# Second self attention of a two-layer transformer kernel: ScalarE seeds the shifted-score banks with the negated maxima, and each fourth slot's score pair stands ahead of its shifted scores

## What is computed

```
q = (h @ wq).reshape(b, n, 16, 64).transpose(0, 2, 1, 3)      # k and v likewise
scores = einsum('bhnd,bhld->bhnl', q, k) * 64 ** -0.5
probs = softmax(scores, axis=-1)
out = einsum('bhnl,bhld->bhnd', probs, v)
return out.transpose(0, 2, 1, 3).reshape(b, n, 1024) @ wo + bo
```

## Time and profile before

| | us |
|---|---|
| runs: median (lowest to highest) | 4218.95 (4212.62 to 4226.44) |
| profiled execution, first to last instruction (its span) | 4217.9 |
| TensorE busy in matmuls | 3909.5 |
| VectorE busy | 2770.9 |
| ScalarE busy | 1839.2 |
| GpSimd busy | 1859.2 |

### The profile page before, as it was taken

One profiled execution on the slowest core, in us unless ns is written; L12 is line 12 of the kernel. 1 busy time (PEld: TensorE's weight loads), 2 busy tenths in 40 slices (PEclk: granted clock), 3 DMA queues, 4 the chain that ended last, 5 costly groups with the idle time before them and its releaser, 6 DMA issues. The chain is left out here.

```text
span 4217.9 us, 64445 instructions
## 1 busy us (share of the span) xinstructions
PE 3909.5 (93%) x24639; PEld 2598.3 (62%) x24639; DVE 2770.9 (66%) x4547; ACT 1839.2 (44%) x2746; POOL 1859.2 (44%) x1203
## 2 busy tenths in 40 slices
PE   3799999994998997998999999999999979999899
PEld 2533443433557886884666666666666647777787
DVE  6599999953536654435676767676766737665665
ACT  1267777771443333442333333333333334444333
POOL 1288970001203002005777777877787753222200
PEclk9789999996779998997999999999999989999899
DMA  4734434405622005883211111121112010000100
GB/s 159 180 56 77 59 57 48 42 2 94 102 43 52 22 13 197 306 308 103 75 51 51 64 63 51 51 76 51 51 51 76 26 31 10 10 10 1 42 15 17
DMA packets 314421, 294.96 MB, mean 70 GB/s; under 512 B 133420, under 2 KB 237292, under 8 KB 313860
## 3 DMA queue, kind: packets, MB, share of 16 engines
q1 hardware_dynamic: 311460, 281.88, 25.7%
q0 software_dynamic: 2656, 8.97, 0.7%
HBM read 161.92 MB, written 127.28 MB: 69 GB/s over the span
## 5 line engine op out<-in xcount | busy, mean ns | idle before, releaser
L1741 POOL TENSOR_TENSOR f_sums<-f_sums,f_probs 128x1024 f32<-128x1024 f32 x384 | 915.5, 2384 | 154.8 <-ACT f_probs L1860 117.1
L1860 ACT ACTIVATE f_probs<-f_st 128x1024 f32<-128x1024 f32 x512 | 525.0, 1027 | 938.7 <-PE f_st L1906 933.9
L1758 DVE TENSOR_REDUCE f_mx<-f_s 128x1 f32<-128x512 f32 x1024 | 659.8, 686 | 380.7 <-PE f_s L1883 369.4
L1369 DVE TENSOR_REDUCE f_mx<-f_s 128x1 f32<-128x512 f32 x1024 | 638.6, 683 | 50.8 <-PE f_s L1501 28.4
L1481 ACT ACTIVATE f_probs<-f_st 128x512 f32<-128x512 f32 x1024 | 535.9, 601 | 225.6 <-PE f_st L1518 225.5
L1883 PE MATMUL f_s<-f_k,f_q 64*128 64x512 f32 x3072 | 515.0, 415 | 18.6 <-DMA f_k<-k 12.5
L1906 PE MATMUL f_st<-f_q,f_k 64*128 64x512 f32 x3072 | 485.2, 390 | 1.1 <-ACT f_probs L1860 1.0
L1920 PE MATMUL f_acc<-f_probs,f_v 128*64 128x512 f32 x2048 | 465.0, 596 | 0.0
L1883 PEld LDWEIGHTS f_s<-f_k,f_q 64*128 64x128 f32 x3072 | 341.2, 189 | 166.6 <-issue 112.1
L1906 PEld LDWEIGHTS f_st<-f_q,f_k 64*128 64x128 f32 x3072 | 366.4, 184 | 25.9 <-ACT f_probs L1860 3.8
L1518 PE MATMUL f_st<-f_q,f_k 50*128 50x512 f32 x1024 | 332.7, 472 | 6.9 <-ACT f_probs L1481 6.8
(11 more groups left out here) (320 smaller groups left out, 7874.5 us busy)
## 6 DMA issues: line engine op xcount, KB each, us to landing
q<-f_stage SPq DMA_DIRECT2D x80, 512.0 KB, 2.9
k<-f_stage SPq DMA_DIRECT2D x80, 512.0 KB, 2.9
f_q<-q SPq DMA_DIRECT2D x32, 1024.0 KB, 5.0
f_k<-k SPq DMA_DIRECT2D x32, 1024.0 KB, 7.3
v<-f_v_stage SPq DMA_DIRECT2D x64, 256.0 KB, 3.1
f_v<-v SPq DMA_DIRECT2D x32, 512.0 KB, 8.5
f_q<-q SPq DMA_DIRECT2D x96, 128.0 KB, 4.2
f_k<-k SPq DMA_DIRECT2D x96, 128.0 KB, 6.9
```

Source lines behind the costliest of these rows:

```text
L1369: v.tensor_reduce(mx[:, i % 2, c:c + 1], bank[u % 4][:, :], AX_X, ALU.max).then_inc(s_free, 1)
L1741: g_.tensor_tensor(out, out, probs[:, n % NP, :, :], ALU.add).then_inc(sum_done, 1)
L1758: v.tensor_reduce(mx[:, i % 2, c:c + 1], bank[u % 3][:, :], AX_X, ALU.max).then_inc(s_free, 1)
L1860: a_.activation(probs[:, s % NP, :, :], stb[s % 2][:, :, :], ACT.Exp, scale=L.scale).then_inc(p_ready, 1)
```

## The change

- `shifted` loses its two matmuls with `mones`. Instead ScalarE writes the negated maxima into the buffer first (`seed`, a copy of 128x1024 from SBUF), and the six matmuls add to it (`start=False`). `seed(n + 2)` stands on ScalarE right behind the exponential of slot n, whose buffer it reuses, and waits for that exponential. `prime` runs four matmuls once, so that the buffers' matmuls add.
- For the seeds the maxima lie on all partitions: VectorE copies them once (`turned`), SyncE's queue writes them to DRAM and, when that has landed, reads them back into all 128 partitions (1 MB, two buffers). `turn` moves from the block after slot 15 to slot `TURN` = 10.
- In each fourth slot (s = 3, 7, 11, 15) the score pair stands ahead of the shifted scores; in the others it stays behind them. So no pair stands behind a block any more. `EARLY` goes from 3 to 7.
- The loads of q and k are split from those of v and wait for the shifted scores of the step before, no longer for its values.

```diff
-        NP, DEPTH, GROUP, EARLY, RING0 = 8, 3, 4, 3, 3
+        NP, DEPTH, GROUP, EARLY, RING0, TURN = 8, 3, 4, 7, 3, 10
...
                 def maxima(i):
                     par = i % 2
-                    sp.wait_ge(m_split, i + 1)
-                    for h in range(2):
-                        for r in range(2):
-                            row = 64 * h + r
-                            sp.dma_start(m[par][row:row + 1, :].bitcast(F32).rearrange("o (q t) -> o q t", t=P),
-                                         mm[par][h * QB:(h + 1) * QB, r, :]).then_inc(m_in[par], 16)
+                    sp.wait_ge(s_free, at["turn", i] + 1)
+                    if i >= 2:
+                        sp.wait_ge(m_in[par], 16 * (i // 2))
+                    sp.dma_start(self.shift[par].rearrange("(c t) -> c t", t=P), mm[par][:, :]).then_inc(m_out[par], 16)
+                    sp.wait_ge(m_out[par], 16 * (i // 2 + 1))
+                    if i >= 2:
+                        sp.wait_ge(seeded, (i - 1) * SLOTS)
+                    sp.dma_start(shift[par][:, :, :].rearrange("p h t -> p (h t)"), self.shift[par].partition_broadcast(P))\
+                        .then_inc(m_in[par], 16)
...
                 for i in range(STEPS):
                     if i + 2 < STEPS:
                         if i > 0:
+                            sp.wait_ge(st_ready, i * SLOTS)
+                        load(i + 2)
+                        if i > 0:
                             sp.wait_ge(pv_done, i * GROUP)
-                        load(i + 2)
+                        load_values(i + 2)
...
+                def seed(n):
+                    i, s = n // SLOTS, n % SLOTS
+                    half = s // KC
+                    if n >= 2:
+                        act.wait_ge(p_ready, n - 1)
+                    if s == 0:
+                        act.wait_ge(m_in[i % 2], 16 * (i // 2 + 1))
+                    a_.activation(stb[s % 2][:, :, :], shift[i % 2][:, :, half * HALF:(half + 1) * HALF], ACT.Copy).then_inc(seeded, 1)
...
                         a_.activation(probs[:, s % NP, :, :], stb[s % 2][:, :, :], ACT.Exp, scale=L.scale).then_inc(p_ready, 1)
+                        if n + 2 < STEPS * SLOTS:
+                            seed(n + 2)
...
                 def shifted(i, s):
-                    cur, par, half, c = i % DEPTH, i % 2, s // KC, s % KC
-                    if s == 0:
-                        pe.wait_ge(m_in[par], (i // 2 + 1) * 64)
-                    pe.wait_ge(p_ready, i * SLOTS + s + 1)
+                    cur, half, c = i % DEPTH, s // KC, s % KC
+                    pe.wait_ge(seeded, i * SLOTS + s + 1)
...
-                    for r, (kk, qq) in enumerate(((0, 0), (0, 1), (1, 0), (None, None))):
+                    for r, (kk, qq) in enumerate(((0, 0), (0, 1), (1, 0))):
...
                     for s in range(SLOTS):
+                        n, j = (i + 1, EARLY + s) if s < SLOTS - EARLY else (i + 2, s - SLOTS + EARLY)
+                        if n < STEPS and s % GROUP == GROUP - 1:
+                            pair(n, j)
                         shifted(i, s)
...
+                        if s == TURN and i + 1 < STEPS:
+                            turn(i + 1)
...
+                        if n < STEPS and s % GROUP < GROUP - 1:
+                            pair(n, j)
```

More of the change, by code:

```diff
@@ L115, in __init__ @@
         self.rden = dram("rden", (B * H, N))
+        self.shift = dram("shift", (2, 2 * N))
         self.wq = {}
@@ L1638, in attend_wide @@
             vs = [sb(f"v{k}", [P, KC, 2, W]) for k in slots_of]
-            m = [sb(f"m{k}", [P, N], F32R) for k in two]
-            mones = sb("mones", [P, P], F32R)
+            shift = [sb(f"shift{k}", [P, 2, N]) for k in two]
             ones = sb("ones", [P, W])
@@ L1645, in attend_wide @@
             negm = sb("negm", [P, 2 * QB])
-            mm = [sb(f"mm{k}", [2 * QB, 2, P]) for k in two]
+            mm = [sb(f"mm{k}", [2 * QB, P]) for k in two]
             on = sb("on", [P, 2, HALF])
@@ L1669, in load @@
                 def load(i):
-                    slot, b, g = i % DEPTH, i // L.ng, i % L.ng
+                    slot = i % DEPTH
                     row = slice(i * P, (i + 1) * P)
@@ L1702, in _ @@
                 g_ = nc.gpsimd
[L1703 to L1709, removed]
                 g_.memset(ones[:, :], 1.0).then_inc(set_done, 1)
@@ L1769, in turned @@
                     if i >= 2:
[L1770 to L1776, removed]
+                        dve.wait_ge(m_out[par], 16 * (i // 2))
+                    v.tensor_copy(mm[par][:, :], rows).then_inc(s_free, 1)
                 def invert(n):
@@ L1818, in _ @@
                             normalise(2 * i)
[L1819 to L1828, removed]
+                        if s == TURN and i + 1 < STEPS:
+                            turned(i + 1)
+                        if s == 15 and i > 0:
+                            project(2 * i - 1)
+                        if n < STEPS and s % GROUP < GROUP - 1:
+                            pair(n, j)
                         if s == SLOTS - EARLY - 1 and i + 1 < STEPS:
@@ L1850, in high @@
                     a_.activation(o_hi[:, half, :], on[:, half, :], ACT.Copy).then_inc(hi_done, 1)
+                act.wait_ge(primed, 1)
+                seed(0)
+                seed(1)
                 for i in range(STEPS):
@@ L1870, in _ @@
                 pe.sem_inc(s_ready, RING0)
[L1871 removed]
+                pe.wait_ge(set_done, 1)
                 def pair(i, j):
@@ L1946, in project @@
                         ins.then_inc(s_ready, 1)
+                prime()
                 for j in range(2 * QB):
@@ L1965, in _ @@
                             values(i, 1)
+                        if s == TURN and i + 1 < STEPS:
+                            turn(i + 1)
                         if s == 15:
-                            if i + 1 < STEPS:
-                                turn(i + 1)
                             if i > 0:
```

29 lines of the change are left out of this document (17 added, 12 removed).

## The result

The changed kernel takes 4291.47 us (median; 4284.74 to 4292.28, four runs), the kernel before, run beside it, 4217.45 (4212.62 to 4226.44, four runs): a ratio of 1.0161, 95% interval 1.0138 to 1.0184. The two matmuls a slot are gone and the program is 74 us longer. The profiled execution is the lowest of the four, 4284.74; its span is 4282.5. The other three lie within 1.1 us of each other, 7 us above it.

A forecast was written before the change was run, and what follows sets the result against it. TensorE's slot (1.62 us) and the three-bank ring's pace (1.64) were taken as equal bounds. Terms 50.4 + 11.7 + 6.9 + 1.1 + 8.0 + 1.9 = 80.0 on 4217.9 gave 4298; own range 4269 to 4327, widened to 4238 to 4342.

The forecast's parts named there:

- the likeliest case: Whole kernel: slower because score pairs wait for the three score banks; 4298 us, 77% chance.
- S2 / P2 / P3 wakes: Group's third shifted scores start at 3.19 us, third score pair at 3.99; fourth pair's second head resumes at 5.63.
- group without pairs: Last groups, no score pairs left: shifted scores wait for seeds, block at 6.10 us, +1.72 a group over 4.38.
- The ring: Three score banks: a pair's second head waits for the previous pair's first VectorE reduction; own pace 0.90 + 0.69 + 0.05 = 1.64.
- The woken pair: Score pair resumed after waiting for a bank: its first reduction starts 0.77 us after its start, not 1.00.
- The seed: ScalarE copy of 128x1024 from SBUF to PSUM: 1.05 us; at the lower end, 0.93, some 20 us less in all.
- The wait: TensorE idles for VectorE's reduction where one score pair follows another: 0.6 to 0.8 us a group, some 100 us.
- GpSimd: GpSimd's work for eight slots takes 18 us of now 24, so it adds nothing to the time.
- The half clock at the start: Stage's start at 1.2 GHz: four more early pairs at 2.01 each cost 8.0 us, `prime` 1.9.
- the first: Rival: the three banks don't hold, ScalarE's chain sets the group, faster at 4159 or 4123 us; 12%.
- nothing waits for a DMA: Judges the rival that the broadcast maxima land late, over 13 us; at 15 us, 62 more, 4360; 4%.
- the granted clock is 1.00: Judges the rival that the clock falls to half, 19 us a step, 57 in three steps, 4355; 2%.

The follow-up runs named there:

- repeated run: The changed kernel, unedited, profiled once more to check the clock at the stage's start: 4293.89 us.
- the half reductions: Changed kernel with each VectorE row maximum over 256 of the 512 keys and the exponential's scale at 0: 4252.49 us, 1.0065 of the kernel before.
- the order alone: Kernel before, matmuls with the maxima kept, no seeds; only the score pair put ahead of the shifted scores in each fourth slot: 4337.59 us, ratio 1.0255.

## Why the prediction was right

4298 us forecast, 4291.47 measured, inside the likeliest case's own range. By its steps, all from the profiles:

| term | forecast | measured |
|---|---|---|
| group, plain | 7.21 (+0.42) | 7.17 (+0.38) |
| S2 / P2 / P3 wakes, from the group's start | 3.19 / 3.99 / 5.63 | 3.15 / 3.95 / 5.59 |
| group with the turn | 7.63 | 7.67 |
| step | 48.5 | 48.5 |
| group without pairs | 6.10 | 6.04 |
| start (4 pairs, `prime`), at half clock | +9.9 | +10.1 |
| the same at full clock for 24 us | not foreseen | +2.6 |
| stage, repeated run / first profile | +80 | +76 / +70 |

The start is the time from the stage's first matmul to the first shifted scores: 1912.71 to 1951.85 before, 1915.42 to 1964.63 in the repeated run of the change, 1907.09 to 1948.78 in its first profile. The stage's length runs to the end of the last addition to x (3436.14; 3515.16; 3500.76).

- *The ring* was read rightly, and all three of its parts held: the first head's reduction 0.90 behind a running pair (2516.31 to 2517.21), 0.69 for one reduction, 0.05 to wake. The price of the order was shown by undoing it, and that of the reduction by shortening it.
- *The woken pair*, worked out from half clock as 0.77 to its reduction, was right too: alone at full clock pairs now come every 1.52, and 0.77 + 0.69 + 0.05 is 1.51.
- *The seed* takes 1.03, not 1.05, and begins 0.03 behind the exponential, not 0.05; S2 is 0.04 earlier, and with it everything behind: that is all of the plain group's miss, some 4 us. The lower end of 0.93 was not reached. Beside the copy SBUF to SBUF in the same profile (1.050, two of them, into another type, fp32r) the seed's 1.029 is 0.02 shorter; the rule of the Trainium skill, page "ScalarE: Activation LUTs", section "ACT is a hardware spline evaluator", agrees in its sign as far as these two can be compared, but that is worth under 3 us and not the 20 weighed against it.
- *The wait* was put at 0.6 to 0.8 and some 100 us in all; the profile shows 0.54 and 64.3. The mechanism and the time at which TensorE goes on are right; the last matmul ahead of the gap starts at 2517.01, 0.94 before the next. The prediction took a couple's 0.23 of that as work, which leaves 0.71; the profile takes that matmul's own 0.42, which leaves 0.52. It changed no term.
- *DMAs* were hidden, as forecast: 1.3 and 4.7 us to land.
- *GpSimd* was put at nothing, and in the loop that held. At the stage's end it did not: the kernel before waits there for GpSimd's last sums,

```profile
3424.90 1.97 PE L1929 MATMUL f_s<-f_sums,f_ones 128*64 128x512 f32 x4 [4.10 <-POOL f_sums L1741]
```

  and the longer groups of the change leave GpSimd more time: the same wait is 0.29 in its first profile and 1.79 in the repeated run. That gives back 2 to 4 us that the forecast doesn't have.
- *The half clock at the start* was assumed for the changed kernel because the kernel before had it. In the profile it had ended after some 3 us and came back 24 us later; 15 pairs by 0.49 in between is the 7 us that separates the two starts (10.1 and 2.6), and the stage lengths differ by 6. The repeated run had the half clock as assumed. That the median lies nearer to the forecast than the profile does is in this respect chance: the level differs between executions, and the three executions without a profile don't show theirs.

Two slips in the prediction's sums change nothing: four groups and four blocks of today are 46.5 us, not 46.4, and 4298 + 18 + 9 is 4325, not 4327.

The rivals: the ring holds, so the first falls by the half reductions; in the loop nothing waits for a DMA; the granted clock is 1.00 from 1975 to 3434 us, with TensorE idle 4% to 5% of it. Only in the groups without pairs, where TensorE waits 1.48 and 1.04 for seeds, is it 0.50 for some 7 us (3436 to 3443) and again for 3 us (3484 to 3487).

## What to carry to other kernels

Where two limits have the same length, here TensorE's slot (1.62) and a ring's passage (1.64), cutting one buys little until the other is cut too: four couples of matmuls a group fewer gave 0.06 us of 0.93 in the old order, three couples fewer 0.19 of 0.70 at best. Count how many passages through a ring lie between two blocks before moving a producer across a block: the block had hidden one pair's passage, and moving that pair cost 0.4 to 0.9 us a group. Work given to an idle engine costs least in the stretch where that engine idles: with the two seeds written around the block (and six early pairs) TensorE has no idle time from 1980 to 3376 us, while the third, between two exponentials, held S2 up. Put it there, and start whatever it depends on early enough: one slot sooner took off 15 us here.

## What the runs showed of the hardware that was not expected

The granted clock at the start of one stage differs between executions of one program. First matmuls of the stage, TensorE, changed kernel, first profile and repeated run:

```profile
1907.09 2.04 PE L1912 MATMUL f_st<-f_q,f_k 128*128 128x512 f32 x4 [12.56 <-DMA f_k<-k]
...
1912.86 1.10 PE L1896 MATMUL f_s<-f_k,f_q 64*128 64x512 f32 x6 [0.42 <-DVE f_mx L1763]
```

```profile
1915.42 2.04 PE L1912 MATMUL f_st<-f_q,f_k 128*128 128x512 f32 x4 [12.44 <-DMA f_k<-k]
...
1921.84 1.65 PE L1896 MATMUL f_s<-f_k,f_q 64*128 64x512 f32 x6 [0.36 <-DVE f_mx L1763]
```

Both wait 12.5 us for the same DMA and then run the same list; the one has 1.00 (2.4 GHz) from 1910.3 to 1934.6, the other 0.50 (1.2 GHz) until 1966. The first one doesn't keep it (windows in the columns of the earlier trace rows):

```profile
1910.00:1930.00 20.00, 14.32 (x81) 8.62 (x78) 16.61 (x26) 2.01 (x2) 9.25 (x3) 0.99 0.43 152
1935.00:1950.00 15.00, 12.83 (x48) 7.21 (x50) 8.99 (x15) 3.25 (x3) 0.00 (x0) 0.50 0.67 245
```

Between the two TensorE stands idle for 1.38 us, waiting for the negated maxima ahead of the stage's first transposition, and the level falls during that wait. Eight profiles were at full clock when they came to that wait of 1.38: in six the level falls during it, in two within 2 us behind it. In the ninth, with the halved reductions, the wait is 0.84 and the level stays at 1.00. No run varied that wait alone.

Of the twelve profiles of this case, seven rose within some 5 us of the stage's first matmul; five, the kernel before among them, stayed at half clock for longer. The two kernels without `prime` (before, and the order alone) are both among the five, the ten with it stand seven to three: too few to say whether `prime` changes the odds, and enough to say that it doesn't decide. It is worth 7 us of 4290 here, half of the 13 us that a measurement of this kernel can tell. What decides the rise stays open.
